# An LSTM ahead of a pipeline of layers: a PSUM bank for each gate in the first eight steps, the output gate's tanh last, and the engines' lists in a new order

## The reference

```python
# LSTM step: four gates, N x 128 each, order i, f, o, g
g  = x[t] @ Wx + h @ Wh + b
c  = sigmoid(f) * c + sigmoid(i) * tanh(g)
h  = sigmoid(o) * tanh(c)
```

## Time and profile before

| | |
|---|---|
| median of 3 runs | 563.84 us (562.88 to 564.41) |
| the profiled execution | 563.99 us |
| its span, first to last instruction | 562.4 us |
| mean granted clock of PE in it | 0.997 |
| PE busy | 542.6 us (96%) |
| DVE busy | 430.8 us (77%) |
| ACT busy | 380.8 us (68%) |
| POOL busy | 196.3 us (35%) |

### The profile page before, as it was taken

One profiled execution on the slowest core, in us unless ns is written; L12 is line 12 of the kernel. 1 busy time (PEld: TensorE's weight loads), 2 busy tenths in 40 slices (PEclk: granted clock), 3 DMA queues, 4 the chain that ended last, 5 costly groups with the idle time before them and its releaser, 6 DMA issues.

```text
span 562.4 us, 10019 instructions
## 1 busy us (share of the span) xinstructions
PE 542.6 (96%) x3341; PEld 469.5 (83%) x3341; DVE 430.8 (77%) x1026; ACT 380.8 (68%) x857; POOL 196.3 (35%) x186
## 2 busy tenths in 40 slices
PE   8999999999999999999999868889999999999997
PEld 7877888887877899999999756779999988888885
DVE  4987655566869788678747338899999999999956
ACT  4567767767766755344633245788888888889975
POOL 4688778778688204938000000000011000000100
PEclk9999999999999999999999999899999999999999
DMA  8633306430090302030000000111101111112121
GB/s 281 189 150 156 151 2 224 188 128 22 4 335 5 131 5 77 1 114 19 2 1 1 0 1 1 20 38 21 20 19 20 20 30 30 29 30 56 29 68 37
DMA packets 30226, 37.35 MB, mean 66 GB/s; under 512 B 20096, under 2 KB 23648, under 8 KB 29280
## 3 DMA queue, kind: packets, MB, share of 16 engines
q1 hardware_dynamic: 30176, 36.72, 20.1%
HBM read 30.24 MB, written 2.28 MB: 58 GB/s over the span
## 4 chain that ended last, share of the span: by engine, by line
PE 82%; DVE 8%; ACT 5%; issue 3%; POOL 2%; DVEq 0%; ACTq 0%
PE bank L325 10%; PE bank L1248 10%; PE bank L327 9%; PE bank L326 9%; PE bank L1656 5%; PE bank L1736 4%; PE bank L1648 4%; PE bank L1680 3%; PE bank L1681 3%; PE bank L1316 2%; POOL hidden_low L387 2%; PE bank L1759 1%; PE bank L1198 1%; ACT gates_t L1774 1%; PE bank L1702 1%
## 5 line engine op out<-in xcount | busy, mean ns | idle before, releaser
L387 POOL TENSOR_TENSOR hidden_low<-hidden,hidden_high 128x512 fp32r<-128x512 f32 x72 | 94.3, 1316 | 25.6 <-ACT hidden_high L372 23.3
L2021 POOL CAST h_high<-h 128x256 fp32r<-128x256 f32 x15 | 6.4, 426 | 209.1 <-ACT h L1833 209.1
L452 ACT ACTIVATE bank<-bank 128x512 f32<-128x512 f32 x56 | 32.6, 583 | 33.6 <-PE bank L327 33.3
L456 DVE TENSOR_TENSOR hidden<-bank,big 128x512 f32<-128x512 f32 x56 | 38.6, 689 | 15.8 <-ACT bank L452 14.6
L1680 PE MATMUL bank<-taps_high,q1T 128*128 128x512 f32 x94 | 45.6, 485 | 1.0 <-DVE tap L1933 0.8
L372 ACT CAST hidden_high<-hidden 128x512 fp32r<-128x512 f32 x70 | 43.0, 615 | 4.6 <-DVE hidden L456 3.1
L1774 ACT ACTIVATE gates_t<-bank,lstm_b_half 128x128 f32<-128x128 f32 x128 | 36.7, 375 | 13.1 <-PE bank L1656 13.0
L325 PE MATMUL bank<-xin_high,sw_high 128*128 128x256 f32 x128 | 43.9, 343 | 0.0
L1648 PE MATMUL bank<-x,lstm_wx 128*128 128x128 f32 x256 | 34.9, 279 | 6.5 <-ACT gates_t L1774 6.0
L1648 PEld LDWEIGHTS bank<-x,lstm_wx 128*128 128x128 f32 x256 | 31.6, 192 | 9.9 <-ACT gates_t L1774 9.0
L1656 PE MATMUL bank<-hL,lstm_wh 128*128 128x128 f32 x256 | 35.5, 283 | 3.2 <-DVE hL L1894 3.2
(11 more groups left out here) (269 smaller groups left out, 1727.4 us busy)
## 6 DMA issues: line engine op xcount, KB each, us to landing
big<-gates_scratch SPq DMA_DIRECT2D x7, 2048.0 KB, 7.6
w<-in_f_w SPq DMA_DIRECT2D x16, 256.0 KB, 6.2
onehot<-topi_scratch SPq DMA_DIRECT2D x8, 512.0 KB, 4.0
outT<-x SPq DMA_DIRECT2D x15, 128.0 KB, 2.1
xT<-in_xT SPq DMA_DIRECT2D x3, 512.0 KB, 7.4
hidden<-in_ffn_w SPq DMA_DIRECT2D x3, 256.0 KB, 5.5
hidden<-in_conv_w SPq DMA_DIRECT2D x3, 256.0 KB, 4.3
xT<-in_xT SPq DMA_DIRECT2D x2, 256.0 KB, 4.1
```

Of the source, the lines that this page charges most:

```text
L387: pool.tensor_tensor(hidden_hl[u % 3][1][:, :], hidden[u % 3][:, :], hidden_hl[u % 3][0][:, :].bitcast(F32), ALU.subtract).then_inc(s_lo, 1)
```

## The change

In the first eight LSTM steps each gate has a bank of its own (the banks of the later layers, which wait for the eighth step), and each gate raises a semaphore of its own, so that ACT can read one gate while PE writes the next. The order of the gates is 0, 1, 3, 2 everywhere, and the output gate's tanh is a function of its own, `tanh_output`, with its own semaphore `c_to`; `gate_products` needs only the other three, `new_h` waits for `c_to` as well. At step 0 the product with `h` is issued ahead of the one with `x`. From step 8 on all four gates share bank 0 again, and `tanh_gates` waits for the last of them. The lists of PE, ACT and DVE are new: the first turns written out, then a loop over turns 8 to 17, then a drain written out. Every call of the old lists is in the new ones once (435 on PE, 500 on DVE; ACT has the 32 `tanh_output` besides its 389, each with one of the four tanh of `tanh_gates`). POOL's and SP's lists are the same.

```diff
-            ps_gates, ps_taps = bank[0], bank[1:3]
+            ps_taps = bank[1:3]
...
+            EARLY = 8
+            GATES = (0, 1, 3, 2)
+
+            def gate_ps(t, q):
+                if t < EARLY:
+                    b = (0, 3, 4 if t == 0 else 6, 5)[q]
+                    return bank[b][:, 0:N]
+                return bank[0][:, q * N:(q + 1) * N]
+
             def gate_x(t):
                 if has(t):
-                    if t:
+                    if t == 0:
+                        pe.wait_ge(s_res, 2 * GROUPS)
+                    else:
                         pe.wait_ge(c_tg, t)
-                    else:
-                        pe.wait_ge(s_res, 2 * GROUPS)
-                    if t == FIRST_STEPS:
+                    if t == 1:
                         all_steps(pe)
-                    for q in range(4):
-                        pe.matmul(ps_gates[:, q * N:(q + 1) * N], lstm_wx[:, q * P:(q + 1) * P], x1[:, t, :],
-                                  start=(q == 0), stop=False, skip_group_check=True)
+                    for q in GATES:
+                        if t and q == (2 if t < EARLY else 0):
+                            pe.wait_ge(c_to, t)
+                        mm = pe.matmul(gate_ps(t, q), lstm_wx[:, q * P:(q + 1) * P], x1[:, t, :],
+                                       start=(0 < t < EARLY or (t > 0 and q == 0)), stop=(t == 0), skip_group_check=True)
+                        if t == 0:
+                            mm.then_inc(c_gate[q], 1)
 
             def gate_h(t):
                 if has(t):
                     if t:
                         pe.wait_ge(c_hL, t)
-                    for q in range(4):
-                        mm = pe.matmul(ps_gates[:, q * N:(q + 1) * N], lstm_wh[:, q * P:(q + 1) * P],
-                                       hL[:, (t - 1) % 2, :], start=False, stop=True, skip_group_check=True)
-                    mm.then_inc(c_gh, 1)
+                    for q in GATES:
+                        mm = pe.matmul(gate_ps(t, q), lstm_wh[:, q * P:(q + 1) * P], hL[:, (t - 1) % 2, :],
+                                       start=(t == 0), stop=(t > 0), skip_group_check=True)
+                        if t:
+                            mm.then_inc(c_gate[q], 1)
...
             def tanh_gates(t):
                 if has(t):
-                    act.wait_ge(c_gh, t + 1)
-                    for q in range(4):
-                        tg = act.activation(gates_t[:, q, :], ps_gates[:, q * N:(q + 1) * N], ACT.Tanh,
-                                            bias=lstm_b_half[:, q:q + 1], scale=0.5)
+                    for q in GATES[0:3]:
+                        act.wait_ge(c_gate[q if t < EARLY else GATES[3]], t + 1)
+                        tg = act.activation(gates_t[:, q, :], gate_ps(t, q), ACT.Tanh, bias=lstm_b_half[:, q:q + 1], scale=0.5)
                     tg.then_inc(c_tg, 1)
+
+            def tanh_output(t):
+                if has(t):
+                    act.wait_ge(c_gate[2], t + 1)
+                    act.activation(gates_t[:, 2, :], gate_ps(t, 2), ACT.Tanh, bias=lstm_b_half[:, 2:3], scale=0.5
+                                   ).then_inc(c_to, 1)
...
                     dve.wait_ge(c_tc, t + 1)
+                    dve.wait_ge(c_to, t + 1)
```

More of the change, by code:

```diff
@@ new lines, in pe_program @@
+                up_tap(5, 2)
+                gate_h(9)
+                turn_y(0)
+                up_tap(6, 0)
+                up_tap(6, 1)
+                turn_h(8)
+                rnn(0)
+                up_tap(6, 2)
+                gate_x(10)
+                down1(1)
+                turn_h(9)
+                gate_h(10)
+                up_tap(7, 0)
+                turn_y(1)
+                up_tap(7, 1)
+                rnn(1)
+                turn_q1(8)
+                turn_q1(9)
@@ new lines, in pe_program @@
+                gate_x(11)
+                down1(2)
+                up_tap(7, 2)
+                gate_h(11)
+                turn_y(2)
+                up_tap(8, 0)
+                up_tap(8, 1)
+                turn_h(10)
+                rnn(2)
+                up_tap(8, 2)
+                up2(0, 0)
+                down1(3)
+                gate_x(12)
+                up_tap(9, 0)
+                gate_h(12)
+                turn_y(3)
+                turn_h(11)
+                up2(0, 1)
@@ L2069, in pe_program @@
[L2069 to L2163, removed]
-                turn_y(23)
-                down2(10)
-                rnn(23)
-                turn_q1(30)
-                turn_q1(31)
                 up_tap(29, 2)
-                value(8)
@@ L2239, in pe_program @@
                 mix_products(14)
+                up_tap(31, 2)
                 leaky(31)
@@ new lines, in act_program @@
+                tanh_rnn(2)
+                tanh_conv(3)
+                tanh_cell(11)
+                gelu(0, 0)
+                scale_y(3)
+                quantise_hs(2)
+                tanh_gates(12)
+                tanh_output(12)
+                gelu(0, 1)
+                tanh_rnn(3)
+                round_h(10)
+                round_hs(6)
+                round_h(11)
+                tanh_cell(12)
+                round_hs(7)
+                store_q1(5)
+                scale_y(4)
@@ L2569, in dve_program @@
[L2569 to L2585 removed]
+                gate_products(0)
@@ new lines, in dve_program @@
+                gate_products(4)
+                inverse_h(1)
+                new_cell(4)
+                conv_next(1)
+                new_h(4)
+                conv_here(1)
+                conv_last(1)
+                gate_products(5)
+                conv_next(2)
+                new_cell(5)
+                conv_here(2)
+                new_h(5)
+                conv_last(2)
+                silu(0)
+                gate_products(6)
+                max_h(2)
+                new_cell(6)
@@ new lines, in dve_program @@
+                silu(1)
+                gate_products(8)
+                inverse_h(3)
+                new_cell(8)
+                max_hs(1)
+                new_h(8)
+                step_hs(1)
+                inverse_hs(1)
+                conv_here(5)
+                conv_last(5)
+                new_x2(0)
+                conv_next(6)
+                gate_products(9)
+                new_cell(9)
+                conv_here(6)
+                new_h(9)
+                conv_last(6)
+                max_h(4)
@@ new lines, in dve_program @@
+                silu(2)
+                step_h(4)
+                new_x2(1)
+                inverse_h(4)
+                max_hs(2)
+                gate_products(10)
+                new_cell(10)
+                conv_next(7)
+                step_hs(2)
+                new_h(10)
+                inverse_hs(2)
+                conv_here(7)
+                conv_last(7)
+                new_x2(2)
+                conv_next(8)
+                gate_products(11)
+                conv_here(8)
+                new_cell(11)
```

720 lines of the change are left out of this document (374 added, 346 removed).

## The result

The changed kernel takes 554.69 us, median of 4 runs (554.63 to 554.79); the kernel before, run beside it on the same chip, 563.36 (562.41 to 564.41). The ratio is 0.9846, 95% interval 0.9826 to 0.9865: 1.5% faster. The forecast was 554.9, range 550.5 to 560.5. The profiled execution has a span of 553.3 us (562.4 before).

What follows compares the result with a forecast made beforehand. PE bounds the steady part; 25 us of the stage are not PE work, lost in the first steps and after gate_h(31). Sum: span 562.4 - 8.4 - 0.6 = 553.4, + 1.6 = 555.0, against the median 554.9 us; range 550.5 to 560.5.

Steps and rivals of the forecast that it cites:

- the fill: Recurrent part up to gate_h(12): time lost falls from 15.7 to 7.3 us, so -8.4, bounds -10.7 and -4.5.
- the drain: After gate_h(31): more work left to cover the last chain, against busy DVE and ACT; -0.6 us, bounds -2.0 and +2.0.
- Step 0 and steps 1 to 4: First LSTM steps: gate_h(0) first, loop 2.91 instead of 3.85, gate_h(5) at 337.5; lost so far 3.0 instead of 8.3 us.
- gate_h(5) to gate_h(12): LSTM steps 5 to 12: DVE is the limit with 30.7 us of work; 33.0 taken instead of 36.2, bounds 30.7 and 36.9.
- Steady turns: Middle of the recurrent part: same instructions in another order, 13.36 us a turn, so 0 and no gain possible.
- (b): Steady turns: odd step comes late to gate_h, PE idles each turn; 0.4 us a turn gives 558.5; chance 0.17.
- Increments: gate_h's semaphore raised for each gate, 96 more in all: taken as 0, by the equal pitches of gate_x and gate_h.
- The clock: PE's clock fall in the windows from 350 to 354 us: 1.5 us put to it, left inside the half taken.
- (a): Steps 5 to 12: DVE stalls as before, only the early lead stays; fill -4.5 to -5.4, drain 0, 559 us; chance 0.17.
- (c): gate_h: each semaphore increment costs PE a 0.03 us stall, 2.9 in all, giving 557.8 us; chance 0.06.
- (d): Fill and drain: better drain (-2) and a fill at DVE's limit (-10.7), giving 551 us; chance 0.10.
- (e): Whole kernel: the change does nothing, only if the loop did not set the early pace; no separate chance given.

Runs made afterwards that it cites:

- the second trace of the kernel before: The unchanged kernel before, profiled once more to see whether the clock falls again near 350 us: stage 240.44 (241.65 in the first trace), 563.09 us in one run.
- twelve early steps: The changed kernel with EARLY = 12 in place of 8, so each gate keeps its own bank until step 11 is read: 554.28 us, ratio to before 0.9846.
- half a max_hs: The changed kernel with max_hs of the first four pairs taken over half of the hidden columns, which alters the computation: 553.99 us, ratio to before 0.984.

## Why the prediction came out, step by step

**The total** was right (554.9, measured 554.69), but partly because two terms were off in opposite senses: the fill gave 9.6 where 8.4 was put (0.5 by gate_h(5), 0.7 after), and the drain cost 1.3 where a gain of 0.6 was put. Their errors are -1.2 and +1.9; layer 0's earlier end, which nothing in the change can claim, gave 0.5, and the small parts between fill and drain 0.3. So the closeness is in part luck. The fill's 9.6 is also counted from a trace with the clock's fall: against the second trace of the kernel before it is 8.5.

**Step 0 and steps 1 to 4: right.** gate_h(1) to gate_h(5) came at 323.96, 327.04, 329.88, 332.96 and 336.51, where 324.6, 327.5, 330.7, 333.6 and 337.5 were put; the steps up to gate_h(4) are 2.84 to 3.08 where the loop was put at 2.91. 0.5 of each lead is layer 0's end. Shown one by one: the banks 0.69 a step (0.68 put), the fourth tanh 0.22 to 0.26 (0.26 put), the order of step 0 0.7.

**gate_h(5) to gate_h(12): size near, limit wrong.** 32.3 where 33.0 was put, inside its bounds of 30.7 and 36.9. The step that failed is "DVE is then the limit, PE is not". It is refuted twice: with one bank for the gates steps 5 to 7 lose 1.7 more, which a limit in DVE would have hidden, and with 1.6 us taken off DVE's work there only 0.4 comes back. DVE was busy 31.6 of 32.3 us, and still its *sum* wasn't the limit; the place of single long operations in its list was. The old lists with all else new lose 2.7 more in this stretch, with max_hs ahead of new_h. (The run changed the three lists as a whole; that it is the place of max_hs is read from the rows, not shown by itself.)

What holds steps 8 to 12, where 2.3 are still lost, is neither the first gate's time (twelve early steps) nor DVE's sum (half a max_hs). The changed kernel's chain of waits in this stretch, in order of time, names a candidate:

```profile
358.84 1.22 DVE hs L1974
...
360.24 0.17 DVE sc L1945
...
360.79 0.36 ACT gates_t L1807
361.15 0.36 ACT v L1820
...
361.55 0.44 PE bank L1690 x2
361.99 0.89 PE bank L1663 x8
```

round_h's scale stands behind the long silu on DVE, round_h behind a tanh on ACT, and turn_q1 (L1690), which needs it, ahead of gate_x(11) in PE's list, so the LSTM's next product waits behind a piece of the net. The rival is DVE's own list, where max_hs stood ahead of products(10) and new_h(10). The run with half a max_hs speaks against it at this step, in its timeline of DVE and PE:

```profile
360.49 0.44 PE L1690 MATMUL bank<-ident,v 128*128 128x128 f32 x2 [0.46 <-ACT v L1820]
...
361.67 0.53 DVE L1927 SCALAR_TENSOR_TENSOR hL<-gates_t,tc 128x128 f32<-128x128 f32 x1 [0.36 <-ACT tc L1813]
...
362.40 1.05 PE L1673 MATMUL bank<-hL,lstm_wh 128*128 128x128 f32 x8
```

There hL is ready at 362.20, before PE comes to gate_h(11), and PE still waits the same 0.46 at turn_q1; the step from gate_h(10) to gate_h(11) is 5.17 instead of 5.22. So for 0.46 of the 2.3 PE's wait at turn_q1 is seen in both traces. No run moved turn_q1; that moving it would give the time back, and what holds the rest, stays open.

**Steady turns: right.** 13.36, nothing waits. Rival (b), the stretched turn, did not come: gate_h of an even step follows that of the odd one after 4.77, and the loop's 4.3 (an estimate of the prediction) fits into it. The new steady order gives nothing either, as put: the old one has the same 13.36.

**Increments: right**, zero.

**Drain: wrong in sign.** "More is left to cover the last chain" (down1(31) with 13.7 behind it instead of 9.5) was true of the list but not of the wait that counts. PE's work after gate_h(31) grew by 1.1 and the time by 2.4; with the old order it is 55.8 in all six traces that have it. The term I had on the other side, DVE and ACT having more to do there, has the right sign (+2.0 was the bound, +1.3 came). The last three waits of PE are the same in both traces (1.7 us in sum, from 547 and from 556 on), so the loss isn't at the end. Ahead of them PE waits more than 0.2 us five times in the new drain and twice in the old one. The longest of each stands here (timelines of PE, the changed kernel and the kernel before):

```profile
514.86 0.49 PE L1722 MATMUL bank<-x,rnn_wx 128*128 128x128 f32 x2 [0.53 <-DVE x L1998]
```

```profile
540.07 0.49 PE L1747 MATMUL bank<-x,leak_wz 128*128 128x128 f32 x2 [0.35 <-DVE x L1970]
```

The five are 1.66 us (0.81 for new_x2's x, 0.85 for ACT's tanh_rnn and gelu), the two 0.57: 1.1 more, against the 1.3 lost. So the new order has rnn, down1 and up2 come to PE before DVE and ACT are done. That one of these calls alone costs it was not tested: the kernels changed the whole order from a point on.

**The clock.** I put 1.5 to its fall and measured 1.2. The changed kernel's traces show no fall in these steps, but neither does the second trace of before, so it is not shown that the change keeps the clock up. In time, three of the changed kernel's four runs have a mean clock of 0.996 and one 1.000, and they lie within 0.16 us: whatever fell there cost it next to nothing. So of the 8.7 us between the medians (563.36 and 554.69) up to 1 is the kernel before's own falls; its runs at 0.999 or above are 7.8 us slower than the changed kernel. The Trainium skill ("TensorE: Matmul & The Clock Gate", What's actually happening) ties the fall to idling before it. The two traces of before have the same gap and differ, so here the gap alone doesn't decide.

**Rivals.** (a) would have had gate_h(12) at 373.5 or later; it is 368.83. (b) and (c) are out, as above. (d) was half true: the fill gained more than forecast, the drain lost. (e) is excluded by the 0.9846.

## What to carry to other kernels

In a recurrent loop a full engine isn't yet the limit: look whether its long operations stand between the loop's links, and test by moving or shrinking one, since a sum near the whole stretch (31.6 of 32.3 here) says nothing by itself. Test an order of calls together with what it was made for: the same lists were worth 2.9 us with the shorter loop, and without it 0.8 together with step 0's order. Split a loop's producer so that the consumer can start on its first quarter only for as long as the loop sets the pace; past that point (step 8 here) it gave nothing. Judge the first turns, the steady turns and the drain of a hand-written order apart, because one new order may gain in one and lose in another, and a join between two orders has a price (3.1 us at step 26, at most 0.9 at step 12).

## What was unexpected of the hardware

- Two traces of one and the same kernel, with the same gap of 1.13 us on PE: in one the granted clock fell to 0.81 and 0.50 over 4 us and the stage took 1.2 longer, in the other it stayed at 1.00. One trace is no evidence for what the clock does in a kernel; over 25 runs the time follows the mean clock, 562.4 us at 0.999 or above and 564.7 at 0.991 to 0.994.
- The same code of layer 0 ended at 319.3 to 321.2 us in the fourteen traces of this study; within the recurrent part, traces with the same order repeat each other to some 0.02 a step. Differences under 1 us are better read in a stage than in the time of the whole.
- 72 increments of a semaphore, each behind a 128x128 matmul, cost nothing that shows: 0.04 us of 233 when they are left out.
